# A Pool memset of 112 columns behind each row gather of a product-key expert layer

## The chip, the cores and the metric

The kernel runs on one core of one Trainium2 chip. The metric is the device time of one execution in microseconds (us). Engines are named PE (matmul; its weight loads are PEld), DVE, ACT, Pool and SP. The core's 16 DMA engines move the data; a gather is a DMA whose descriptors Pool writes from a list of row numbers in SBUF.

## The reference

Tokens are 2 x 2048 with 512 features. First comes cross attention over 77 keys, then a product-key expert layer, which is nearly all of the time. Its core:

```python
q = jnp.einsum('bnd,de->bne', x, w_q)               # then batch norm over the tokens
q = q.reshape(b, n, 2, H, KD).transpose(2, 0, 1, 3, 4)
sim = jnp.einsum('pbnhd,hkpd->pbnhk', q, keys)      # 8 heads, 2 x 128 keys
sx, ix = jax.lax.top_k(sim[0], TOPK)                # TOPK = 8
sy, iy = jax.lax.top_k(sim[1], TOPK)
...                                                 # the best 8 of the 64 sums
indices = jnp.take_along_axis(all_indices, pk, axis=-1)
wd = down_embed[indices]                            # 64 rows of 512 per token
wu = up_embed[indices]
h = jnp.einsum('bnd,bnhkd->bnhk', x, wd)
h = jax.nn.softmax(scores, axis=-1) * gelu_new(h)
out = jnp.einsum('bnhk,bnhkd->bnd', h, wu)
```

All is float32. The table has 16384 rows; the kernel holds `down_embed` and `up_embed` side by side, so that a row is 1024 floats, 4 KB.

## The kernel before

`xattn_peer` calls `attention_block`, which ends some 500 us in, and then `expert_block`, which the change touches. The 4096 tokens are 32 tiles of 128 tokens (one token per partition). For each tile each token needs 64 rows; they come in 16 half heads (`HALVES`) of four rows (`HALF`). One gather brings one row for each of the 128 partitions, 512 KB, so there are 32 x 16 x 4 = 2048 gathers, all on Pool (L793). A half head has the number n = 16 t + j, and its four gathers are numbered k.

The buffers hold 36 rows per partition: `rows` has 32 places and `expert_more_rows` four, which makes nine groups (`GROUPS = 9`) of one half head each. The gathers of half head n go to group n mod 9, and Pool first waits on `up_done` until PE is through with half head n - 9. Before each gather Pool also waits on `asked`, which a gather raises once its descriptors are written: gather number i waits until gathers 0 to i - 2 have been through that. So nothing but free places and Pool's own pace holds the gathers back.

What happens to a half head once it has landed: DVE multiplies the four rows' first halves by the normed token (L978), ACT sums each product (L1194) and applies the gelu (L1200), DVE makes coefficients (L984) and four diagonal matrices of them (L992), and PE adds the four rows' second halves, weighted, into a PSUM bank (L1382, two passes for each float32 matmul, so eight rows of the trace per half head). In between, DVE and PE work out the choice of rows for the next tiles. SP loads and stores one token tile for each 64 gathers.

Seven small arrays, `gamma`, `beta`, `var`, `mean_q`, `rs`, `scale` and `offset`, each of 16 columns (`NM`), serve the batch norm in the setup of the block. The last of their readers is ACT, whose work `amat_done` tells of; Pool waits for that at n = 6 (L777 is Pool's own use of them).

```python
if n >= GROUPS:
    wait(pool, "up_done", n + 1 - GROUPS)
...
for k in range(HALF):
    at = j * HALF + k
    if n * HALF + k > 1:
        pool.wait_ge(asked, n * HALF + k - 1)
    gather = pool.indirect_dma_start(...)
```

Of the kernel before, what the change touches and what calls it, by code (L numbers as in the profile page):

```python
# [31 lines left out]
P = 128  # L32
# [9 lines left out]
NM = 2 * PH  # L42
# [15 lines left out]
HALF = TOP // 2  # L58
HALVES = NPICK // HALF
GROUPS = SLOTS // HALF + 1  # L60
# [3 lines left out]
def xattn_peer(nc, x, x_T, ctxT, mask, wq, bq, wk, bk, wv, bv, v_keep, wo, bo,  # L64
# [4 lines left out]
    with ExitStack() as persistent:  # L69
# [50 lines left out]
        with ExitStack() as own:  # L120
            expert_block(nc, maker(own, "expert_"), banks, table, x2_dram, out_v, keysT, gammaT, betaT,
                         rows, wq2, wq2T, cov, mu_row, junk, q_norm, amat, bias_row, ones,
                         ident, minus_half, mean_var2, rstd2, w_in)
# [521 lines left out]
def expert_block(nc, make, banks, table, x2_dram, out_v, keysT, gammaT, betaT, rows, wq2, wq2T, cov,  # L645
# [3 lines left out]
    sb, ps, sem = make  # L649
    X2_RING = 4  # L650
    NQ = NM // 4
    gamma = sb("gamma", [P, NM])
    beta = sb("beta", [P, NM])
    var = sb("var", [P, NM])
    mean_q = sb("mean_q", [P, NM])
    rs = sb("rs", [P, NM])
    scale = sb("scale", [P, NM])
    offset = sb("offset", [P, NM])
    more_rows = sb("more_rows", [P, HALF, 2 * D])
    keys_sb = more_rows[:, :, :].rearrange("p s n -> p (s n)")[:, 0:QD]  # L660

    def four(n):

        g = n % GROUPS
        return more_rows if g == GROUPS - 1 else rows[:, g * HALF:(g + 1) * HALF, :]
# [40 lines left out]
    ev = {n: sem(n) for n in """xn_done turned xnT_done scored seeded topped early_done shifted  # L706
        exp_done idx_done multiplied summed ident_kept gelu_done coef_done diag_done up_done y_done consts yw_done var_done
        mean_done var_eps rs_done scale_made offset_made offset_done raw_done normed scaled bias_done
        bias_kept a_done amat_done flagged offset_wide cov_kept act_kept mu_kept
        squared""".split()}  # L710

    def wait(eng, name, count):
        if not isinstance(count, int) or count > 0:
            eng.wait_ge(ev[name], count)
# [13 lines left out]
    with nc.Block() as block:  # L728
        @block.sync
        def _(sp):  # L730
            sp.dma_start(gamma[:, :], gammaT).then_inc(keys_in, 16)
            sp.dma_start(beta[:, :], betaT).then_inc(keys_in, 16)
            sp.dma_start(keys_sb[:, :], keysT).then_inc(keys_in, 16)

            def load(t, par, half):
                sp.dma_start(x2_t[:, bass.ts(ring(t, par, half), D)], x2_dram[t])\
                  .then_inc(x2_in[par], 16)

            def store(t, par, half):
                wait(sp, "y_done", t + 1)  # L740
                sp.dma_start(out_v[t], x2_t[:, bass.ts(ring(t, par, half), D)])\
                  .then_inc(y_out[par], 16)

            load(0, 0, 0)
            load(1, 1, 0)

            sp.wait_ge(x2_in[0], 16)
            load(2, 0, 1)


            sp.wait_ge(x2_in[1], 16)
            load(3, 1, 1)
            store(0, 0, 0)
            with sp.Fori(0, NT // 2 - 2) as half:
                for par in range(2):
                    t = half * 2 + par
                    if par == 0:
                        store_t, store_half = t + 1, half
                    else:
                        store_t, store_half = t + 1, half + 1  # L760

                    sp.wait_ge(y_out[par], (half + 1) * 16)
                    load(t + 4, par, half + 2)
                    store(store_t, 1 - par, store_half)
            for t in range(NT - 3, NT):
                store(t, t % 2, t // 2)
            for par in range(2):
                sp.wait_ge(y_out[par], 16 * (NT // 2))

        @block.gpsimd  # L770
        def _(pool):
            pool.iota(iota_u[:, :], pattern=[[1, TOP]], base=0, channel_multiplier=0)\
                .then_inc(ev["consts"], 1)
            for q in range(NM // 4):
                some = slice(4 * q, 4 * q + 4)
                wait(pool, "var_eps", q + 1)
                pool.tensor_tensor(rs[:, some], var[:, some], minus_half[:, some], ALU.pow)\  # L777
                    .then_inc(ev["rs_done"], 1)

            for n in range(NT * HALVES):  # L780
                t, j = divmod(n, HALVES)
                if j % (HALVES // 2) == 0:
                    wait(pool, "idx_done", t * 2 + j // (HALVES // 2) + 1)
                if n >= GROUPS:
                    wait(pool, "up_done", n + 1 - GROUPS)
                if n == 6:
                    wait(pool, "amat_done", NM)
                pool.sem_inc(issued, 1)
# [4 lines that stand above are left out]
                    gather = pool.indirect_dma_start(  # L793
                        four(n)[:, k, :], None, table[:, :],
                        bass.IndirectOffsetOnAxis(ap=idx[:, t % 2, at:at + 1], axis=0),
                        engine_sem=asked)
                    if n == LAST:
                        gather.then_inc(last_row_in[k], 16)
                    else:
                        gather.then_inc(row_in[n % GROUPS], 16)  # L800

        @block.vector
        def _(dve):
# [677 lines left out]
```

## Time and profile before

| what | value |
|---|---|
| median of 3 runs | 3226.52 us (3225.11 to 3228.2) |
| the profiled execution: its time, its span | 3225.07 us, 3223.2 us |
| PE, DVE, ACT, Pool busy, share of the span | 89%, 75%, 57%, 66% |
| gathers | 2048, of 512 KB each; 1073.87 MB in all |
| first and last gather start | 532.4 us, 3183.6 us |
| granted TensorE clock, mean | 0.979 of full speed |

The span runs from the first instruction to the last of the profiled execution; 1.9 us of its time lie outside. Times inside it are counted from its start. "Busy" on Pool is the time that the trace gives its instructions; a gather counts as busy while its descriptors are written, not while the data moves. "To landing" is the time from the start of a gather on Pool to the last of the 16 DMA engines' reports.

### The profile page before, as it was taken

To read this page: it belongs to the slowest core of one execution; us is meant where nothing else is said; L and a number is where in the kernel's file an instruction comes from. 1 tells how busy PE (TensorE), PEld (TensorE's weight loads), DVE (VectorE), ACT (ScalarE), POOL (GpSimd) and SP (SyncE) were. 2 spreads that over 40 slices of the span, in tenths; PEclk is the share of its full clock that TensorE was granted. 3 is DMA by queue.
4 is the path that set the end of the run, shared out by engine and by line. 5 is a ranking of instruction groups with operands and counts; after the bars stand their busy time and mean duration, and the time that the engine had idled before them with its cause. 6 is when DMAs were issued, how large, how long until landed. Compare 5 with 4: busy or idle time off the path is not lost.

```text
span 3223.2 us, 36101 instructions
## 1 busy us (share of the span) xinstructions
PE 2869.0 (89%) x10310; PEld 1376.2 (43%) x10310; DVE 2408.6 (75%) x5229; ACT 1821.2 (57%) x5592; POOL 2141.0 (66%) x2224
## 2 busy tenths in 40 slices
PE   8999999998888888888898888888888888888877
PEld 6777767433333333333333333333333333333322
DVE  5888716977777777777777777777777777777765
ACT  3566503665565555655556555555556555565555
POOL 1555513777777777777777777777777777777773
PEclk9999999999999999999999999999999999999999
DMA  6222103999999999999999999999999999999996
GB/s 228 78 70 76 38 30 138 412 412 411 412 412 411 412 412 412 411 412 412 412 411 412 412 412 412 412 411 410 411 411 406 411 409 412 404 412 403 412 411 254
DMA packets 324861, 1133.07 MB, mean 352 GB/s; under 512 B 36331, under 2 KB 36971, under 8 KB 324024
## 3 DMA queue, kind: packets, MB, share of 16 engines
q0 software_dynamic: 294912, 1073.87, 83.2%
q1 hardware_dynamic: 29088, 56.41, 4.9%
q8 instruction: 82, 1.34, 0.2%
q10 hardware_dynamic: 664, 0.50, 0.1%
q14 instruction: 115, 0.94, 0.1%
HBM read 1113.87 MB, written 16.78 MB: 351 GB/s over the span
## 4 chain that ended last, share of the span: by engine, by line
DMA 56%; PE 13%; issue 9%; DVE 4%; POOL 2%; ACT 0%; POOLq 0%; ACTq 0%; DVEq 0%
DMA rows<-in_table,expert_idx 51%; PE banks L1382 9%; DMA expert_more_rows<-in_table,expert_idx 5%; POOL rows L793 2%; PE banks L1371 2%; PE banks L1306 1%; DVE expert_top_i L901 1%; DVE expert_diag L992 1%; DVE expert_top_s L893 1%; DVE rows L978 1%; PE banks L1318 0%; DVE expert_coef L984 0%; PE banks L1347 0%; DVE expert_best_i L924 0%; POOL expert_more_rows L793 0%
## 5 line engine op out<-in xcount | busy, mean ns | idle before, releaser
L793 POOL DMA_INDIRECT rows<-in_table,expert_idx x1824 | 1725.1, 946 | 655.1 <-DMA rows<-in_table,expert_idx 512.0
L1382 PE MATMUL banks<-rows,expert_diag 128*128 128x512 f32 x3640 | 1714.5, 616 | 289.0 <-DVE expert_diag L992 288.5
L1194 ACT ACTIVATE rows<-rows 128x512 f32<-128x512 f32 x1820 | 1121.8, 617 | 939.0 <-DVE expert_coef L984 936.9
L978 DVE TENSOR_TENSOR rows<-rows,banks 128x2048 f32<-128x2048 f32 x455 | 1040.9, 2288 | 551.3 <-DMA rows<-in_table,expert_idx 551.3
L1382 PEld LDWEIGHTS banks<-rows,expert_diag 128*128 128x128 f32 x3640 | 687.9, 195 | 1266.9 <-issue 751.8
L1371 PE MATMUL banks<-amat,expert_xnT 128*128 128x512 f32 x992 | 465.6, 593 | 3.7 <-ACT banks L1185 3.0
L992 DVE TENSOR_TENSOR expert_diag<-banks,expert_coef 128x512 f32<-128x512 f32 x511 | 348.0, 681 | 0.7
L1194 ACT ACTIVATION_READ_ACCUMULATOR rows<-rows 128x1 f32 x1820 | 339.3, 186 | 0.0
L1371 PEld LDWEIGHTS banks<-amat,expert_xnT 128*128 128x128 f32 x992 | 188.5, 190 | 240.5 <-issue 228.7
L793 POOL DMA_INDIRECT expert_more_rows<-in_table,expert_idx x224 | 212.4, 948 | 85.2 <-DMA expert_more_rows<-in_table,expert_idx 47.9
L1382 PE MATMUL banks<-expert_more_rows,expert_diag 128*128 128x512 f32 x448 | 216.5, 629 | 38.9 <-DVE expert_diag L992 38.9
L1194 ACT ACTIVATE expert_more_rows<-expert_more_rows 128x512 f32<-128x512 f32 x224 | 138.1, 617 | 110.8 <-DVE expert_coef L984 110.8
L978 DVE TENSOR_TENSOR expert_more_rows<-expert_more_rows,banks 128x2048 f32<-128x2048 f32 x56 | 128.1, 2288 | 62.0 <-DMA expert_more_rows<-in_table,expert_idx 61.8
L1382 PEld LDWEIGHTS banks<-expert_more_rows,expert_diag 128*128 128x128 f32 x448 | 86.6, 199 | 162.5 <-issue 96.0
L257 POOL TENSOR_TENSOR attention_rstd<-attention_var_eps,minus_half 128x1 f32<-128x1 f32 x32 | 17.9, 559 | 197.4 <-DVE attention_var_eps L316 197.4
L437 ACT ACTIVATE attention_prob_pad<-attention_prob_pad,attention_neg_max 128x77 f32<-128x77 f32 x512 | 140.4, 347 | 8.1 <-DVE attention_neg_max L340 6.2
L901 DVE FIND_INDEX8 expert_top_i<-expert_top_s,banks 128x8 uint32<-128x128 f32 x512 | 139.2, 291 | 0.0
L498 PE MATMUL banks<-attention_xT_t,amat 128*128 128x128 f32 x1024 | 128.7, 280 | 0.7 <-DVE attention_prob_pad L336 0.7
L446 ACT ACTIVATE attention_probT<-banks 128x512 f32<-128x512 f32 (+1 forms) x96 | 47.1, 524 | 138.8 <-PE banks L513 136.6
L538 PE MATMUL banks<-amat 128*128 128x512 f32 x256 | 123.2, 605 | 0.0
L498 PEld LDWEIGHTS banks<-attention_xT_t,amat 128*128 128x128 f32 x1024 | 120.3, 193 | 6.8 <-issue 6.8
L893 DVE MAX8 expert_top_s<-banks 128x8 f32<-128x128 f32 x512 | 113.5, 285 | 3.1 <-PE banks L1371 3.1
(133 smaller groups left out, 2099.7 us busy)
## 6 DMA issues: line engine op xcount, KB each, us to landing
rows<-in_table,expert_idx POOLq DMA_INDIRECT x1824, 14.8
attention_xT_t<-in_x_T SPq DMA_DIRECT2D x32, 256.0 KB, 3.1
attention_x_t<-in_x SPq DMA_DIRECT2D x32, 256.0 KB, 3.0
x_dram<-rows SPq DMA_DIRECT2D x32, 256.0 KB, 2.0
expert_x_t<-x_dram SPq DMA_DIRECT2D x32, 256.0 KB, 6.1
out_y<-expert_x_t SPq DMA_DIRECT2D x32, 256.0 KB, 6.1
rows<-in_w_q SPq DMA_DIRECT2D x4, 1024.0 KB, 6.2
rows<-in_w_qT SPq DMA_DIRECT2D x4, 1024.0 KB, 8.4
```

What stands on the lines that cost most here:

```text
L437: ins = act.activation(prob[:, t % 2, h, :], prob[:, t % 2, h, :], ACT.Exp, bias=neg_max[:, t % 2, h:h + 1])
L446: act.activation(probT[:, r, 0:n], banks[:, PROBT_BANK + r % 2, 0:n], ACT.Copy)\
L498: mm = pe.matmul(banks[:, Q_BANK, j * P:(j + 1) * P], attn_w[:, 0, c, j * P:(j + 1) * P], xT_t[:, t % XT_RING, c, :], start=(c == 0), stop ...
L538: mm = pe.matmul(out_ps, attT[:, c, :], attn_w[:, 1, c, :], start=(c == 0), stop=(c == KC - 1))
L793: gather = pool.indirect_dma_start(four(n)[:, k, :], None, table[:, :], bass.IndirectOffsetOnAxis(ap=idx[:, t % 2, at:at + 1], axis=0), en ...
L893: ins = dve.max(top_s[:, m * TOP:(m + 1) * TOP], score_ps[:, q % 2, i * NK:(i + 1) * NK])
L901: ins = dve.max_index(top_i[:, h // HH, m % 2, h % HH, :], top_s[:, m * TOP:(m + 1) * TOP], score_ps[:, q % 2, i * NK:(i + 1) * NK])
L978: return dve.tensor_tensor(down, down, xn_ps[:, par, :].unsqueeze(1).to_broadcast([P, HALF, D]), ALU.mult)
L992: dve.tensor_tensor(diag[:, j % RING, :, :], ident_ps.unsqueeze(1).to_broadcast([P, HALF, P]), coef[:, j % RING, :].unsqueeze(2).to_broadc ...
L1194: ins = act.activation(down, down, ACT.Copy, accum_out=hid[:, j % RING, k:k + 1])
L1371: mm = pe.matmul(score_ps[:, q % 2, :], xnT[:, par, c, :], amat[:, c, q * 512:(q + 1) * 512], start=False, stop=(c == KC - 1), skip_group_ ...
L1382: mm = pe.matmul(out_ps[:, par, :], diag[:, j % RING, k, :], four(t * HALVES + j)[:, k, D:2 * D], start=(j == 0 and k == 0), stop=(j == HA ...
```

## The change

Behind each gather from half head 9 on, which is 2048 - 36 = 2012 times, Pool writes zeros to a place of 128 partitions x 112 columns. Nobody reads it from then on. So that this place exists without more memory, the seven arrays of the setup become seven slices of one array of 7 x 16 columns. A new semaphore, `paced`, orders each memset behind the one before.

```diff
-    gamma = sb("gamma", [P, NM])
-    beta = sb("beta", [P, NM])
-    var = sb("var", [P, NM])
-    mean_q = sb("mean_q", [P, NM])
-    rs = sb("rs", [P, NM])
-    scale = sb("scale", [P, NM])
-    offset = sb("offset", [P, NM])
+    setup = sb("setup", [P, 7 * NM])
+    gamma, beta, var, mean_q, rs, scale, offset = (setup[:, i * NM:(i + 1) * NM] for i in range(7))
...
-        squared""".split()}
+        squared paced""".split()}
...
                         gather.then_inc(row_in[n % GROUPS], 16)
+                    if n >= GROUPS:
+
+                        wait(pool, "paced", (n - GROUPS) * HALF + k)
+                        pool.memset(setup[:, :], 0.0).then_inc(ev["paced"], 1)
```

On PE, DVE, ACT and SP the instructions stand as they did. On Pool, this is the passage from half head 8 to half head 9 in the kernel before; `expert_idx_done` tells that the row numbers are there, `expert_up_done` that PE is through with a group, `expert_asked` that descriptors are written:

```order
L793 DMA expert_more_rows<-in_table,expert_idx 128x1024 [waits expert_idx_done,expert_asked]
L793 DMA expert_more_rows<-in_table,expert_idx 128x1024 [waits expert_asked] x3
L793 DMA rows<-in_table,expert_idx 128x1024 [waits expert_up_done,expert_asked]
L793 DMA rows<-in_table,expert_idx 128x1024 [waits expert_asked] x3
L793 DMA rows<-in_table,expert_idx 128x1024 [waits expert_up_done,expert_asked]
```

The same place of the changed kernel:

```order
L788 DMA expert_more_rows<-in_table,expert_idx 128x1024 [waits expert_idx_done,expert_asked]
L788 DMA expert_more_rows<-in_table,expert_idx 128x1024 [waits expert_asked] x3
L788 DMA rows<-in_table,expert_idx 128x1024 [waits expert_up_done,expert_asked]
L799 MEMSET expert_setup 128x112
L788 DMA rows<-in_table,expert_idx 128x1024 [waits expert_asked]
L799 MEMSET expert_setup 128x112 [waits expert_paced]
L788 DMA rows<-in_table,expert_idx 128x1024 [waits expert_asked]
L799 MEMSET expert_setup 128x112 [waits expert_paced]
```

No gather has moved against another; between each two of them there is now a memset, and the pattern goes on to the end of Pool's program.

## Rows read from the trace of the kernel before

**Rows 1.** The page, part 2: 40 equal slices of the span, busy tenths.
```profile
POOL 1555513777777777777777777777777777777773
...
DMA  6222103999999999999999999999999999999996
GB/s 228 78 70 76 38 30 138 412 412 411 412 412 411 412 412 412 411 412 412 412 411 412 412 412 412 412 411 410 411 411 406 411 409 412 404 412 403 412 411 254
```
**Rows 2.** The page, part 4: the chain that ended last, by engine.
```profile
DMA 56%; PE 13%; issue 9%; DVE 4%; POOL 2%; ACT 0%; POOLq 0%; ACTq 0%; DVEq 0%
```
**Rows 3.** The page, part 5: busy us, mean ns of one | idle before, releaser.
```profile
L793 POOL DMA_INDIRECT rows<-in_table,expert_idx x1824 | 1725.1, 946 | 655.1 <-DMA rows<-in_table,expert_idx 512.0
L978 DVE TENSOR_TENSOR rows<-rows,banks 128x2048 f32<-128x2048 f32 x455 | 1040.9, 2288 | 551.3 <-DMA rows<-in_table,expert_idx 551.3
```
**Rows 4.** Timeline of Pool from 577 us: start us, duration us, [idle before].
```profile
577.69 0.94 POOL L793 DMA_INDIRECT rows<-in_table,expert_idx  x1 [0.30 <-DMA expert_more_rows<-in_table,expert_idx]
578.93 0.94 POOL L793 DMA_INDIRECT rows<-in_table,expert_idx  x1 [0.30 <-DMA rows<-in_table,expert_idx]
580.17 0.94 POOL L793 DMA_INDIRECT rows<-in_table,expert_idx  x1 [0.30 <-DMA rows<-in_table,expert_idx]
581.41 0.94 POOL L793 DMA_INDIRECT rows<-in_table,expert_idx  x1 [0.30 <-DMA rows<-in_table,expert_idx]
```
**Rows 5.** Groups by line, Pool, 578 to 950 us: busy, mean ns | idle before.
```profile
L793 POOL DMA_INDIRECT rows<-in_table,expert_idx x266 | 251.5, 946 | 81.2 <-DMA rows<-in_table,expert_idx 76.9 <-DMA expert_more_rows<-in_table,expert_idx 2.7 <-PE banks L1382 1.5
L793 POOL DMA_INDIRECT expert_more_rows<-in_table,expert_idx x32 | 30.2, 944 | 9.8 <-DMA expert_more_rows<-in_table,expert_idx 7.3 <-DMA rows<-in_table,expert_idx 2.4
```
**Rows 6.** The same, 950 to 3180 us.
```profile
L793 POOL DMA_INDIRECT rows<-in_table,expert_idx x1524 | 1441.2, 946 | 538.2 <-DMA rows<-in_table,expert_idx 425.3 <-PE banks L1382 69.3 <-issue 24.6
L793 POOL DMA_INDIRECT expert_more_rows<-in_table,expert_idx x188 | 178.4, 949 | 74.2 <-DMA expert_more_rows<-in_table,expert_idx 39.7 <-DMA rows<-in_table,expert_idx 14.4 <-PE banks L1382 10.7
```
**Rows 7.** Timeline of Pool, the memsets of the program's first 3 us.
```profile
0.29 0.10 POOL L1472 MEMSET const-float32-1.0<- 128x1 f32 x1
0.32 0.10 POOL L1472 MEMSET const-bfloat16-1.0<- 128x1 bf16 x1
...
0.74 0.20 POOL L284 MEMSET ident<- 128x128 f32 x1 [0.29 <-POOLq L1472]
0.88 0.11 POOL L285 MEMSET minus_half<- 128x16 f32 x1
...
1.56 0.51 POOL L292 MEMSET bias_row<- 128x512 f32 x1
2.02 0.19 POOL L293 MEMSET bias_row<- 128x128 f32 x1
```
**Rows 8.** Stretches: us, PE, PEld, DVE, ACT, POOL busy, PEclk, DMA share, GB/s.
```profile
600.00:700.00 100.00, 97.21 (x228) 42.25 (x227) 85.25 (x186) 68.71 (x211) 75.61 (x80) 1.00 1.03 411
1000.00:1500.00 500.00, 436.07 (x982) 183.05 (x981) 385.56 (x846) 297.25 (x912) 360.41 (x384) 0.98 1.03 412
```
**Rows 9.** All of line 793: duration ns min/median/max, first and last start.
```profile
L793 POOL DMA_INDIRECT rows<-in_table,expert_idx x1824: 932/937/1407, 532.4 to 3183.6; - x183
...
DMA to landing us min/median/max: 4.4/14.8/30.2
```
**Rows 10.** Line 793 again, the gathers of 540 to 600 us alone.
```profile
DMA to landing us min/median/max: 6.6/7.8/9.1
```
**Rows 11.** The chain of work in order of time, at the end: start us, us, what.
```profile
3176.12 0.95 DMA rows<-in_table,expert_idx
3177.07 0.29 issue
3177.37 0.94 DMA rows<-in_table,expert_idx
3178.31 0.29 issue
3178.61 27.71 DMA rows<-in_table,expert_idx
```

## Prediction, written before the changed kernel was run

> **What bounds the kernel now.** I read the slices of the span first. From the seventh slice (about 540 us) to the last one the DMA engines are busy throughout and move 403 to 412 GB/s [rows 1]. A gather of 0.524 MB lasts 1.27 us at 412 GB/s; with the load and store of a token tile per 64 gathers it is 1.29 us. The chain that ended last is DMA for 56% and PE for 13% [rows 2], and DVE's wait for landed rows, 551 us, is long [rows 3]. So the DMA engines bound the gather phase.
>
> Pool comes next and is close. Where nothing holds it, gathers start every 1.24 us: 0.94 us of writing descriptors and 0.30 us of gap [rows 4]. The gap is put down to a DMA, but it is 0.30 us at every gather, whatever the backlog is, so I take it as a fixed cost of each gather. From 578 to 950 us, 298 gathers took 251.5 + 81.2 + 30.2 + 9.8 = 372.7 us, 1.2507 us each, and PE's buffers held Pool for 1.5 us only [rows 5]. That is Pool's own pace, with the now and then longer gather (up to 1.4 us, [rows 9]) in it. It is faster than the DMA engines', so a backlog grows: landing takes 6.6 to 9.1 us at 540 to 600 us [rows 10], 14.8 us in the median of all [rows 9], and 27.7 us at the end [rows 11]. From 950 us on the 36 places are full of waiting rows and Pool is held back: 1712 gathers in 1441.2 + 538.2 + 178.4 + 74.2 = 2232.0 us, 1.3037 us each [rows 6]. **Pool's slack is therefore 1.3037 - 1.2507 = 0.053 us per gather.** Everything hangs on whether a memset costs Pool more than that.
>
> **The change part by part.** *Removed:* nothing. *Moved:* the seven arrays into one; the same instructions on the same columns, in a setup that ends before the gathers fill the places, no cost either way. The place isn't read once `amat_done` is in, so the memsets delay nobody by their data. *The new wait* on `paced` is for a memset that stands a whole gather (0.94 us) earlier, so it has long ended; behind it on Pool stands only the next gather, and the price is in the bounds below.
>
> *Added:* 2012 memsets. No memset stands next to a gather in the trace, so I bound one. Timed from start to start, a 128-column memset holds Pool for 0.88 - 0.74 = 0.14 us and a 512-column one for 2.02 - 1.56 = 0.46 us, and a one-column one for 0.03 us [rows 7]. The slope is 0.32/384 = 0.00083 us a column, so 112 columns hold Pool for 0.14 - 16 x 0.00083 = 0.127 us. By the recorded durations, 0.19 to 0.20 us for 128 columns [rows 7], it would be 0.19 us if the next gather waits until the last byte has landed. The lower end is 0: the 0.30 us gap between two gathers [rows 4] may be work of Pool's sequencer, beside which a memset of 0.13 us would fit. The upper end is 0.19 us and a second gap of 0.30 us, 0.49 us, if the gap belongs to every change from one instruction to another. A gain from the memset itself is excluded, since it takes no work away; a gain from what its pace does is a rival below. I take 0.127 us: memsets in a row run so, each starting before the recorded end of the one ahead, and I see no row in which Pool did another instruction's work within a gap.
>
> Pool's recorded durations give 0.19 us and the starts 0.127 us. The Trainium skill, Perfetto Trace Analysis, section GPSIMD Engine Instruction, says to time Pool's instructions by the spacing of their starts and not by their durations, which would make the sum 3367 us and not 3494 us; it also has the descriptors written by two of Pool's own cores, each of which works its queue in order, which speaks for a memset that lengthens the period.
>
> With 0.127 us a period is 1.2507 + 0.127 = 1.378 us. That is longer than the DMA engines' 1.29 and than what the buffers allow, 1.304, so **Pool becomes the bound** and the slack of 0.053 us is used up first. The other engines follow: at 1.378 a half head has 5.51 us, against 87% and 77% of 5.2 us that PE and DVE need now [rows 8]. The sum, on the profiled execution: gather 36, the first with a memset behind it, starts at 577.7 us [rows 4] in both kernels. 2011 periods of 1.3777 us are 2770.6 us, so the last gather starts at 3348.3 us instead of 3183.6 [rows 9]: +164.7 us. The end gives some of it back. Now 39.6 us follow the last gather's start (3223.2 - 3183.6), 27.7 of them until landing [rows 11] and 11.9 of work. With Pool as the bound there is no backlog; landing is then between the least in the trace, 4.4 us [rows 9], and 6.6 us, with a light backlog [rows 10]. I take 5 us, so 17 us follow: -22.6 us. Outside the span lie 1.9 us: 3348.3 + 17 + 1.9 = **3367 us**, +142 us or 4.4%. The profiled execution (3225.07) lies 1.5 us under the median of the runs, which I leave out.
>
> In short, the total is 577.7 + 2011 x period + 19 us; 0.01 us more or less of memset is 20 us. The kernel comes out as it was at a period of 1.307 us, a memset of 0.056 us.
>
> **The rivals.**
> *The memset lies in the gap.* If the next gather is made ready during the 0.30 us and the memset runs beside that, Pool's pace stays at 1.25 to 1.28 us, under 1.304. The DMA engines stay the bound and nothing moves: 3226 us, within 6. For it: the gap is twice the memset's length. Against it: two gathers never overlap by any part of the gap [rows 4], which looks like work of the engine itself.
> The Trainium skill, DMA: Bandwidth & Descriptors, section Anatomy of one DMA, gives a fixed dispatch of some 50 ns and a small cost for descriptors. By that Pool would have most of each period free, and the sum would be today's 3225 us. The trace disagrees: 0.94 us per gather, and never under 1.24 us from start to start.
>
> *A slower Pool helps.* This is the one that ends on the other side. Now the DMA queues are flooded, and the last gather lands 27.7 us after its start [rows 11] against 7.8 us in the median at 540 to 600 us [rows 10]. At a cost of 0.03 to 0.05 us (that of a one-column memset, [rows 7]) Pool's pace would be 1.28 to 1.30 us, just that of the DMA engines: they would stay fed, and the backlog at the end would be gone. That gives 3225 - (27.7 - 7.8) = 3205 us. It decides at a memset under 0.056 us. Against it: the rate is 411 GB/s with a short backlog and 412 with a long one [rows 8], so data arrive no sooner for a shorter queue, and the DMA engines have then no spare time to make the last rows land earlier, unless a few of the 16 lag behind the rest.
>
> *The next gather waits for the memset's last byte:* 0.19 us, a period of 1.4407, 577.7 + 2897.2 + 18.9 = 3494 us.
> *A second gap:* 0.49 us, a period of 1.74, 4097 us.
> That the change isn't what it says is ruled out: the memsets stand in Pool's order between each two gathers.
>
> **How the numbers follow.** Pool as the bound with 0.10 to 0.16 us per memset (3313 to 3434 us): 0.46. With about 0.19 us (to 3510 us): 0.17. More, up to the second gap: 0.05. In the gap, no change: 0.23. A slower Pool helps: 0.09. The likeliest gives 3367 us, its own range is 3313 to 3434. For 8 in 10 the range must take in the case of the gap and that of 0.19 us: 3215 to 3510 us. It leaves out the second gap and most of the faster case. A measurement of this kernel tells about 0.2%, 6 us, from no change. Faster 0.09, within 0.2% 0.22, slower 0.69.
>
> **What the changed profile would show.** If I am right: Pool's gathers start every 1.37 to 1.38 us from 578 us on to the end, with hardly an idle time that PE ends; the memset group x2012; GB/s in the slices down from 412 to about 0.524/1.378 = 380 plus the tiles' 6; landing near 5 us in the median and not 14.8; DVE's wait for rows longer than 551 us. The number is wrong by 20 us for each 0.01 us of memset. The prediction falls if starts of gathers are still 1.24 us apart in the stretch of [rows 4] (the gap hides the memset), if the slices still show 412 GB/s, or if the gather itself, 0.94 us, has become longer or shorter with a memset beside it.

## The result: 1.1% slower, a quarter of what was forecast

The changed kernel takes 3259.9 us in the median of 4 runs (3258.3 to 3261.9), the kernel before 3225.8 us in the median of 4. The ratio is 1.0107, with a 95% interval of 1.0091 to 1.0123. The forecast was 3367 us, +142; measured are +34 us. The profiled execution of the changed kernel took 3261.33 us, its span is 3259.5 us.

The page of the changed kernel, parts 2 and 4: busy tenths in 40 slices, GB/s, and the chain that ended last by engine. They answer to [rows 1] and [rows 2].

```profile
POOL 1555513888888888888888888888888888888887
...
GB/s 226 77 74 75 34 30 163 407 406 405 400 401 400 403 405 403 402 403 402 407 403 405 401 400 405 401 402 398 404 400 402 403 404 401 404 403 403 402 402 344
...
POOL 69%; issue 10%; PE 3%; DMA 2%; DVE 1%; POOLq 0%; ACT 0%
```

The chain has moved from the DMA engines (56% before) to Pool (69%), and the DMA engines' rate has fallen from 412 to some 403 GB/s. So Pool is the bound, as forecast, but only just: the forecast for the slices was some 386 GB/s.

The timeline of Pool in the changed kernel, where the first memsets stand (start us, duration us, idle before). It answers to [rows 4]:

```profile
578.86 0.94 POOL L788 DMA_INDIRECT rows<-in_table,expert_idx  x1 [0.30 <-DMA expert_more_rows<-in_table,expert_idx]
579.79 0.22 POOL L799 MEMSET expert_setup<- 128x112 f32 x1
580.17 0.95 POOL L788 DMA_INDIRECT rows<-in_table,expert_idx  x1 [0.17 <-issue]
581.12 0.20 POOL L799 MEMSET expert_setup<- 128x112 f32 x1
581.49 0.95 POOL L788 DMA_INDIRECT rows<-in_table,expert_idx  x1 [0.17 <-issue]
```

From one gather's start to the next it is now 1.32 us, where it was 1.24 and 1.37 to 1.38 had been forecast. The memset begins when the gather ends, and from its end it is 0.17 us to the next gather, not 0.30: part of the memset lies in what was the gap.

Pool's groups by line in the changed kernel, 950 to 3180 us (busy us, mean ns | idle before), which answer to [rows 6]:

```profile
L788 POOL DMA_INDIRECT rows<-in_table,expert_idx x1496 | 1424.0, 952 | 247.2 <-issue 246.4 <-PE banks L1381 0.8
L799 POOL MEMSET expert_setup<- 128x112 f32 x1684 | 352.1, 209 | 1.1
L788 POOL DMA_INDIRECT expert_more_rows<-in_table,expert_idx x188 | 178.4, 949 | 31.2 <-issue 30.7 <-PE banks L1381 0.5
```

PE's buffers held Pool for 0.8 + 0.5 us; before it was 69.3 + 10.7. The sum, 1424.0 + 352.1 + 178.4 + 247.2 + 1.1 + 31.2 = 2234.0 us for 1684 gathers, is 1.3266 us each, against 1.3037 before. Line 788 of the changed kernel as a whole, answering to [rows 9], and the end of its chain, answering to [rows 11]:

```profile
L788 POOL DMA_INDIRECT rows<-in_table,expert_idx x1824: 933/943/1471, 533.6 to 3242.1; - x183
...
DMA to landing us min/median/max: 4.6/6.0/8.2
```
```profile
3236.83 5.74 DMA rows<-in_table,expert_idx
3242.63 2.17 issue
```

The last gather starts at 3242.1 us, 58.5 us later than before. 17.4 us follow it, where 39.6 did: -22.2 us. 58.5 - 22.2 = 36.3 us, which is the difference of the spans (3259.5 - 3223.2). So the time came from Pool's period and went back in part through the short backlog. One small thing moved beside them: the median recorded length of a gather is 0.943 us, where it was 0.937 [rows 9]. This 0.006 us is within the period of 1.32 us.

### The profile page after: what moved, and what is told of

The parts are those of the page before. It is cut to its first block, busy times and chain, and to the rows that moved or that the text cites. A ratio compares the mean times of both kernels' runs of the same rounds, so it can differ in the third digit from the quotient of the medians.

```text
span 3259.5 us, 38113 instructions
## 1 busy us (share of the span) xinstructions
PE 2872.6 (88%) x10310; PEld 1374.6 (42%) x10310; DVE 2408.6 (74%) x5229; ACT 1821.4 (56%) x5592; POOL 2568.6 (79%) x4236
## 4 chain that ended last, share of the span: by engine, by line
POOL 69%; issue 10%; PE 3%; DMA 2%; DVE 1%; POOLq 0%; ACT 0%
POOL rows L788 50%; POOL expert_setup L799 12%; POOL expert_more_rows L788 6%; DMA rows<-in_table,expert_idx 2%; PE banks L1381 2%; PE banks L1305 1%; PE banks L1317 0%; POOLq L783 0%; DVE expert_top_i L900 0%; DVE expert_top_s L892 0%; DVE expert_diag L991 0%; PE banks L1424 0%; PE banks L1370 0%; DMA expert_more_rows<-in_table,expert_idx 0%; DVE expert_best_i L923 0%
## 5 line engine op out<-in xcount | busy, mean ns | idle before, releaser
L799 POOL MEMSET expert_setup<- 128x112 f32 x2012 | 420.6, 209 | 1.3
L1381 PE MATMUL banks<-expert_more_rows,expert_diag 128*128 128x512 f32 x448 | 208.0, 608 | 40.0 <-DVE expert_diag L991 40.0
```

The lines of the kernel that those rows point to most:

```text
L799: pool.memset(setup[:, :], 0.0).then_inc(ev["paced"], 1)
L1381: mm = pe.matmul(out_ps[:, par, :], diag[:, j % RING, k, :], four(t * HALVES + j)[:, k, D:2 * D], start=(j == 0 and k == 0), stop=(j == HA ...
```

## The experiments

Twelve runs follow, of eight different kernels, in three groups of four, each group on one chip beside its own runs of the kernel before. On the first two chips the kernel before took 3570 and 3546 us, and gathers moved some 362 and 366 GB/s. The third was like that of the prediction, 3225 us and 411 GB/s. What Pool does between two gathers is the same on all three, within 0.004 us.

**A. The law of the memset: 1, 64, 80, 224 and 280 columns.** The edit is the size alone; over 112 columns the place is an array of its own.

```diff
-                        pool.memset(setup[:, :], 0.0).then_inc(ev["paced"], 1)
+                        pool.memset(setup[:, 0:1], 0.0).then_inc(ev["paced"], 1)
```

> The memset behind each gather clears 1 column instead of 112. Theory A, the memset's start-up lies beside the tail of the gather ahead and only its columns lengthen the period: the 0.074 us of 112 columns less 111 x 0.00083 us is below nothing, so Pool's pace stays near 1.25 us from 578 to 950 us, the DMA engines stay the bound and the time is that of the kernel before, 3226 us within 6. Theory B, 0.074 us is the fixed price of having any other instruction between two gathers: pace 1.32 us and 3260 us, as with 112 columns.

Measured on the first chip: 3578.9 us against 3570.1, ratio 1.0025 (1.0016 to 1.0034). The timeline of Pool with 1 column:

```profile
1499.57 0.94 POOL L788 DMA_INDIRECT rows<-in_table,expert_idx  x1 [0.19 <-issue]
1500.51 0.11 POOL L799 MEMSET expert_setup<- 128x1 f32 x1
1500.81 0.94 POOL L788 DMA_INDIRECT rows<-in_table,expert_idx  x1 [0.19 <-issue]
```

The gathers start 1.24 us apart, as without a memset: a short memset costs Pool nothing at all. Theory B, a fixed price for any instruction in between, is refuted. Why the whole is 0.25% slower on that chip these rows don't tell; it stays open.

> 64 columns. Theory A: 0.074 - 48 x 0.00083 = 0.034 us, a pace of 1.285 us where Pool is free, a little faster than the DMA engines' 1.29 to 1.30 us; the backlog grows slowly and PE's buffers hold Pool only near the end. With a helpful pace about 3200 us, limited by 1092 MB at 412 GB/s (2650 us from 533 us on, and 12 us behind it: 3197 us); without, 3226 us. Theory B: 3260 us.

Measured on the first chip: 3574.8 against 3570.1 us, ratio 1.0012 (1.0003 to 1.0022); median period of Pool 1.273 us. The total is again a little above the kernel before, and less so than with 1 column.

> 80 columns. Theory A: 0.074 - 32 x 0.00083 = 0.047 us per memset, a pace of 1.298 us; Pool bounds just before the DMA engines do. If a slower Pool helps, as the third rival of the prediction has it: 577.7 + 2011 x 1.298 + 19 = 3207 us, landing 6 to 10 us at the end. If it does not, since the DMA engines are full at 1.30 us anyway: 3226 us within 6. Theory B: 3260 us.

Measured on the first chip: 3570.9 against 3570.1 us, ratio 1.0006 (0.9997 to 1.0015); median period 1.292 us.

> 224 columns, in a place of their own. Theory A: 0.074 + 112 x 0.00083 = 0.167 us, a pace of 1.418 us, 578.9 + 2011 x 1.418 + 19 = 3449 us. Theory B, a fixed price: 3260 us. A third one, C: the next gather waits for the memset's last byte and a fixed 0.17 us behind it, which also grows by the columns: as theory A.

Measured on the first chip: 3552.5 against 3570.1 us, ratio 0.9952 (0.9937 to 0.9967), so faster; median period 1.408 us. The median period follows theories A and C, the time none of them. The mean period was (3531.3 - 592.2)/2011 = 1.461 us (592.2 and 3531.3 us are the starts of the first and the last gather with a memset behind it), so on this chip something other than Pool's own pace holds the gathers back, even with 224 columns. D comes back to it.

> 280 columns: 0.072 + 168 x 0.00083 = 0.211 us by the law, a mean period of 1.2507 + 0.211 = 1.462 us, with 577.7 + 2011 x 1.462 + 19 = 3537 us as the least it can take. On a chip with 365 GB/s that is just the DMA engines' pace (before: 3546 to 3570 us): H, an even pace helps up to the point where Pool becomes the bound, gives 0 to 0.7% faster, less than with 224 columns if stalls come on top. At 412 GB/s: 3537 us and some, 9.6% slower.

Measured on the third chip: 3547.1 against 3224.8 us, ratio 1.1000 (1.0982 to 1.1019), 10 us over the 3537 expected. The timeline of Pool with 280 columns:

```profile
1499.63 0.94 POOL L789 DMA_INDIRECT rows<-in_table,expert_idx  x1 [0.17 <-issue]
1500.58 0.35 POOL L800 MEMSET expert_idle_place<- 128x280 f32 x1
1501.09 0.95 POOL L789 DMA_INDIRECT rows<-in_table,expert_idx  x1 [0.17 <-issue]
```

Together, medians in us over the gathers from half head 9 on. The rows for no memset and 112 columns are the kernels before and after; the others are the first chip's, and 280 columns the third's:

| columns | gather | memset | its end to next gather | gather's end to next gather | period |
|---|---|---|---|---|---|
| none | 0.937 | - | - | 0.305 | 1.243 |
| 1 | 0.937 | 0.113 | 0.191 | 0.305 | 1.243 |
| 64 | 0.943 | 0.165 | 0.163 | 0.329 | 1.273 |
| 80 | 0.947 | 0.179 | 0.165 | 0.345 | 1.292 |
| 112 | 0.943 | 0.205 | 0.165 | 0.371 | 1.315 |
| 224 | 0.943 | 0.298 | 0.165 | 0.464 | 1.408 |
| 280 | 0.943 | 0.345 | 0.165 | 0.511 | 1.455 |

The time from a gather's end to the next one's start is the greater of 0.305 us and the memset's recorded length plus 0.165 us. Counted by the recorded length, 0.14 us of the gap can be shared with a memset and 0.165 cannot. This is also what theory C says: the next gather starts a fixed time behind the memset's recorded end, only that this fixed time is a part of the old gap and doesn't come on top of it. Counted as the prediction did, by how long a memset holds Pool among other memsets (0.127 us for 112 columns), the shared part is 0.127 - (0.371 - 0.305) = 0.06 us. Both counts fit all sizes, since the two lengths differ by some 0.08 us at 1 and at 112 columns alike; these runs can't tell them apart. From 112 to 280 columns a column costs (1.455 - 1.315)/168 = 0.00083 us, the slope that was read from the setup's memsets. A memset of one column is free. Carried down from the larger sizes, the slope makes it free up to some 25 to 35 columns; this is an estimate, as no run lies between 1 and 64.

**B. One part of the change alone.**

```diff
-                    if n >= GROUPS:
-
-                        wait(pool, "paced", (n - GROUPS) * HALF + k)
-                        pool.memset(setup[:, :], 0.0).then_inc(ev["paced"], 1)
```

> The seven small arrays in one place, and no memset: one part of the change alone. All theories: the time of the kernel before within 0.2%, Pool's pace 1.25 us. Only if the places in SBUF mattered would it move.

Measured on the second chip: 3545.8 against 3545.9 us, ratio 0.9998 (0.9989 to 1.0007), Pool's median period 1.243 us. So the places in SBUF don't matter on this chip. On the third one this part didn't run alone, but the kernel with 80 columns has it too and takes as long as the kernel before (below). All of the change's effect is the memsets'.

**C. Does a slower Pool help?** This was the rival on the other side. The edit is again the size.

> 80 columns again, since the chip of the first four runs moved some 360 GB/s and not 412. There the starts of two gathers were 1.243 us apart with 1 column, 1.273 with 64, 1.292 with 80 and 1.408 with 224: from about 25 columns on a column costs 0.00083 us. On a chip with 412 GB/s, where the kernel before takes 3226 us, that law gives 80 columns a memset of 0.046 us and a mean period of 1.2507 + 0.046 = 1.297 us: 577.7 + 2011 x 1.297 + 19 = 3205 us if the DMA engines keep up with an even pace (theory H, a slower Pool helps), 3226 us if they do not (theory N, full is full).

Measured on the second chip: 3548.8 against 3545.9 us, ratio 1.0007 (0.9999 to 1.0016). One of its 12 executions took 16443 us, and why isn't known. That chip moves 366 GB/s, so this told nothing of 412.

> 64 columns on the same chip as the 80. The law gives 0.031 us and a mean period of 1.282 us, under what the DMA engines do at 412 GB/s (1.292 with the tiles). H: 3197 to 3215 us, a backlog that grows slowly. N: 3226 us. Where the chip moves 360 GB/s: no change from the kernel before, within 0.2%, as in the first look at 64 columns.

Second chip: 3546.6 against 3545.9 us, ratio 1.0005 (0.9997 to 1.0014).

> 80 columns, for a chip with 412 GB/s if this is one: 3205 us if an even pace just at the DMA engines' own helps (H), 3226 us if not (N). On a chip of the other kind: no change, as twice before.

Third chip: 3226.2 against 3224.8 us, ratio 1.0003 (0.9993 to 1.0012). This is the decisive one. The page's rate and the landing with 80 columns there:

```profile
GB/s 220 86 70 70 44 30 127 412 412 411 410 412 411 409 412 411 409 412 409 411 408 410 410 411 411 412 409 410 410 411 410 411 409 411 410 411 411 409 410 278
```
```profile
DMA to landing us min/median/max: 4.5/7.1/22.8
```

Pool ran at its own, even pace (1.298 us in the mean, and PE's buffers held it for 3.6 us in all), the median landing fell from 14.8 to 7.1 us, and the total didn't move: the rate stayed at 408 to 412 GB/s. Theory N holds.

The median hides why. The gathers have queue 0 of the DMA engines. Here is what it did after the last gather's start, first in the kernel before (3199 to 3211 us), then with 80 columns (3202 to 3212 us), as packets, MB and share of 16 engines' time:

```profile
q0 software_dynamic: 85, 0.31, 6.3%
```
```profile
q0 software_dynamic: 71, 0.26, 6.3%
```

A share of 6.3% of 16 engines is one engine at full work. So at the end a single DMA engine of the 16 lags behind the rest. In the kernel before the first 15 reports on each of the last four gathers come within 14.7 us of its start and the 16th at 27.7; with 80 columns within 10.5 us and at 21.2. A backlog of this kind grows along the run at Pool's pace of 1.298 us too: the longest landing with 80 columns is 12.3 us between 1000 and 1100 us and 22.1 us between 3000 and 3100 us, with a median of 7.2 and 6.7. A half head can be used only when its last report is in, so by these landings it is the slowest engine that bounds the kernel before, at (3183.6 + 27.7 - 577.7 - 7.8)/2011 = 1.306 us per gather (an estimate; 7.8 us is the landing at the start, [rows 10]), against 1.29 us by the mean rate of all 16. The same reckoning gives 1.305 us with 80 columns, and 1.305 in the run that follows. A slower Pool can't help as long as that engine is never idle, and the last landing comes at 3211 us in one kernel and 3212 in the other. Which engine it is, and why it lags, isn't known.

> No memset. Instead Pool waits, before the gathers of half head n, until those of half head n - 4 have landed, so that at most 16 gathers are under way. It tells what helped on the chips with 365 GB/s. Theory Q, the short queue is what helps: a gain like that of 224 columns, 0.5 to 0.7%, there, and 0 to 0.6% at 412 GB/s, with Pool's pace within a half head still 1.24 us. Theory S, the spacing of single gathers helps: no gain, or a loss where the wait leaves the quick DMA engines without work behind the slow ones.

```diff
                 if n >= GROUPS:
                     wait(pool, "up_done", n + 1 - GROUPS)
+                    pool.wait_ge(row_in[(n - 4) % GROUPS], ((n - 4) // GROUPS + 1) * 64)
```

This edit is made in the kernel before. Third chip: 3223.7 against 3224.8 us, ratio 0.9998 (0.9989 to 1.0008). Here no memset runs, the wait bounds the backlog (median landing 7.3 us, longest 17.4), and the time is again the same. The slowest engine is still behind: the last gather's report comes 15.7 us after its start, at 3208 us. So neither way makes its queue empty, and neither helps at 412 GB/s. The question this run was written for, what helps on the other kind of chip, it could not answer, since it ran on the third.

**D. One kernel, both signs.**

> 224 columns: 0.165 us by the law, a mean period of 1.2507 + 0.165 = 1.416 us. At 412 GB/s Pool is the bound by far: 577.7 + 2011 x 1.416 + 19 = 3444 us. At 360 GB/s, where a gather takes the DMA engines 1.46 us, it stays under their pace: 0.5% faster than before, as in the first look. One kernel, both signs, set by which side the DMA engines' pace lies.

Measured on the second chip: 3518.4 against 3545.9 us, ratio 0.9926 (0.9911 to 0.9940). So 224 columns give 0.5% and 0.7% on the two slower chips; by the law of the table and the run with 280 columns they would cost some 7% on the third (3444 us, an estimate), which wasn't tried. The stretches of the run without memsets (first) and with 224 columns (second) on the second chip (us, PE, PEld, DVE, ACT, POOL busy, PEclk, DMA share, GB/s):

```profile
1000.00:3000.00 2000.00, 1609.10 (x3518) 686.46 (x3517) 1367.14 (x3028) 1058.94 (x3261) 1298.42 (x1373) 0.91 0.96 366
```
```profile
1000.00:3000.00 2000.00, 1640.90 (x3549) 687.56 (x3550) 1381.83 (x3045) 1067.34 (x3288) 1745.06 (x2777) 0.93 0.98 370
```

There the DMA engines have idle time (shares of 0.96 and 0.98, against 1.03 in [rows 8]), and it is a little less with the spaced gathers. That their own pace is the bound on these two chips, as the expectations take it, is therefore not shown: the kernel with 280 columns on the third chip, where Pool is the bound, has a share of 0.98 as well. The traces there also hold only part of the landings' reports, so waits for rows can't be read from them.

They do show something else. ACT's gelu waits for one semaphore only, `summed`, which ACT's own instruction just ahead of it raises. Its group in the kernel before (L1200), in the run without memsets on the second chip (L1195 there) and with 224 columns on that chip (L1200), with busy us, mean ns | idle before:

```profile
L1200 ACT ACTIVATE expert_act_h<-expert_hid 128x4 f32<-128x4 f32 x511 | 105.0, 205 | 15.4
```
```profile
L1195 ACT ACTIVATE expert_act_h<-expert_hid 128x4 f32<-128x4 f32 x511 | 105.0, 205 | 434.6 <-remote 290.5 <-issue 114.7 <-ACT rows L1189 16.8
```
```profile
L1200 ACT ACTIVATE expert_act_h<-expert_hid 128x4 f32<-128x4 f32 x511 | 105.0, 205 | 24.1 <-ACT rows L1194 6.7 <-remote 1.5 <-issue 0.4
```

On the slower chips an engine thus stands idle for up to 9.6 us before an instruction for which, by the program, no rows and no other engine are missing, and with the memsets of 224 columns nearly all of this is gone: 434.6 us fall to 24.1 on the second chip. So slow data alone don't explain these chips, and this may be where the gain of 224 columns comes from. How much of the time hangs on it is not shown; spacing and a shorter queue come together in this run, and no run on such a chip took them apart. Whether the chip, or something else at work beside the kernel, makes the difference isn't known either.

> The change as it is, beside the others on one chip. Its pace of 1.32 us is slower than the DMA engines at 412 GB/s (1.29) and faster than at 365 GB/s (1.46). So: 1.0% slower than before on a chip of the first kind (3260 against 3226 us), between no change and 0.4% faster on one of the second kind.

Measured on the third chip: 3266.6 against 3224.8 us, ratio 1.0130 (1.0113 to 1.0147), so the result repeats on another run of the change a little larger than at first (1.0091 to 1.0123). Pool's median period is 1.315 us both times.

## Why the prediction was right in direction and wrong in size

**The bound and the slack.** Right in number. Pool's pace alone, 1.2507 us, and the 0.053 us of slack are what decided: 80 columns cost 0.045 us on the third chip (0.049 in the table) and changed nothing, 112 columns cost 0.072 us and did. What sets the other side is narrower than the prediction says: not the 16 DMA engines at 1.29 us per gather but the slowest of them at 1.306. The slack came out well because it was taken from the stretch in which Pool waits for just that engine (1.3037 us), through PE's buffers. The reading of [rows 1] is off by a slice: the seventh still shows 138 GB/s, the full rate begins with the eighth, at 564 us.

**The memset's price.** This is the step that failed. The prediction took 0.127 us, the time a 112-column memset holds Pool among other memsets, and put all of it on top of the gap of 0.30 us. Measured are 0.072 us in the median, and by the means (3242.1 - 578.9)/2011 - 1.2507 = 0.0736 us. 0.006 us of this are the longer gather, which the prediction had named as a sign against it and which is small. The slope had been read well, 0.00083 us a column. What was missing is that part of the memset runs in the gap. With 0.0736 in the prediction's own formula the total is 577.7 + 2011 x 1.3243 + 19 = 3259.9 us, and the runs gave 3259.9: the mis-sized term, 0.0534 us x 2011 = 107 us, is all of the error. That it fits to 0.1 us is in part luck. The period is read from the changed kernel itself, the first such gather started 1.2 us later than in the kernel before, and 19.2 us came behind the last one, which gives 3261.3 us; that is the profiled execution, and it lies 1.5 us over the median.

**The cases.** The prediction knew of both mechanisms, a memset within the gap (0 to 0.03 us) and one behind it (0.127 us), and treated them as alternatives. Its cases stepped from 0.056 to 0.10 us with nothing between. It used the lack of overlap between two gathers as evidence that the gap is the engine's own work throughout; the table shows that, by the recorded lengths, this holds for 0.165 us of it and not for 0.14. Two instructions of one kind, both with the gap, can't show what another kind may share of it. The measured time lies outside the likeliest case's own range (3313 to 3434 us). It lies within the wide range only by luck, because the ends of two other cases enclosed it; no case forecast it.

**The end.** Right: 17 us were forecast after the last gather, 17.4 measured, so the backlog's 22 us did come back. The median landing was forecast near 5 us and is 6.0. With Pool at 1.324 us, over the slowest engine's 1.306, that engine keeps up too: the longest landing of all is 8.2 us.

**Starts or recorded lengths.** The Trainium skill, Perfetto Trace Analysis, section GPSIMD Engine Instruction, says to time Pool's instructions by the spacing of their starts and not by their recorded durations. The runs agree in part: the spacing of a 112-column memset among other memsets gave 0.127 us, nearer to the measured 0.072 than the 0.19 us by the durations, but neither is right, since the spacing must be taken beside the neighbours that the instruction will have. The slope is the same by both, (0.345 - 0.205)/168 = 0.00083 us a column by the durations. What the Trainium skill says on the same page of the queues of Pool's own cores was read in the prediction as speaking for no overlap with the gap; the runs show overlap.

**The rivals.** "In the gap" was half right. "A slower Pool helps" is refuted at 412 GB/s, by 80 columns and by the wait on landed rows. The prediction had named the weak point, "unless a few of the 16 lag behind the rest": one does, and its backlog at the end is real, but as it had work throughout in these runs, a slower Pool didn't make its last rows land earlier. On the two chips that moved 360 to 370 GB/s the 224-column kernel was faster than before. Of "the next gather waits for the last byte" only the price, 0.19 us on top of the old gap, is refuted; the order fits, since the next gather starts 0.165 us behind the memset's recorded end. "A second gap" is refuted by the periods in the table.

## What to carry to other kernels

Before work is added to an engine that is not the bound, compute its own period where nothing holds it and compare it with the period of the bound: here the margin was 4%, though the engine's busy share was 66%. The price of an instruction put between two others is its length less what it can share of the gap between them, which two runs measure, one with a one-column and one with a large instruction. Where two mechanisms give two prices, the mixture of both is a case too, and the range between them should not be left empty. A median over many transfers can hide one DMA engine that lags: look at the longest landing and at how it changes along the run.

## What the runs showed of the hardware that was not expected

- Of the 0.305 us between two gathers on Pool, 0.14 us by the recorded length can be filled with a memset at no cost. From 64 columns on, 0.163 to 0.165 us remain between a memset's recorded end and the next gather (five sizes, three chips).
- The same kernel before took 3225, 3546 and 3570 us on different chips, at 411, 366 and some 362 GB/s between 1000 and 3000 us (the last two from the runs without memsets and with one column). Whether an edit of Pool's pace helps or hurts depended on the chip: 224 columns gave -0.5% and -0.7% on the slower two, 280 columns +10% on the fastest.
- On the slower two, ACT stood idle for up to 9.6 us before an instruction that waits only for ACT's own semaphore, 434.6 us in all without memsets and 24.1 with 224 columns; on the fastest it was 15.4.
- At 412 GB/s one DMA engine of the 16 lags: it needs 1.306 us per gather (an estimate from the landings), the mean rate 1.29. In two ways the landing fell from 14.8 to 7.1 and 7.3 us in the median and the total stayed within 0.1%, because this engine had work throughout and the last landing stayed at 3208 to 3212 us.
